# A graph network on Trainium2: gathered rows added by two engines, SiLU gives the slot back, and a new order of the stages

## The chip, the cores and the metric

The kernel runs on one core of a Trainium2 chip. The metric is the device time of one execution in microseconds (us). The engines are named as in the profile: PE (TensorE, matmuls; PEld are its weight loads), DVE (VectorE), ACT (ScalarE), POOL (GpSimd) and SP (SyncE, which starts DMAs).

## What is computed

Two layers of message passing on a graph of 6250 nodes with 128 features and 100000 edges, sorted by destination. Layer 1 is the part that matters here:

```python
src, dst = (edge_index[0], edge_index[1])
msg_input = jnp.concatenate([h[src], h[dst], edge_feat], axis=-1)
messages = jax.nn.silu(msg_input @ W1 + b1) @ W2 + b2
agg = jax.ops.segment_sum(messages, dst, num_segments=h.shape[0])
upd_in = jnp.concatenate([h, agg], axis=-1)
h_new = jax.nn.silu(upd_in @ W3 + b3) @ W4 + b4
return h_new + h
```

The result is added to x and normalised (a layer norm). Layer 2 sums x[src] over the edges of each node, sends the sum through a small network and normalises again. All of it is float32.

## The kernel before

**Tiling.** Nodes lie in 49 tiles of 128. Edges lie in 196 groups of 512, and two groups make a pair: 98 pairs. The product h @ W1 for the source part is computed once for all nodes and stored in memory as a table (src_term); a group's 512 rows of it are then gathered by four indirect DMAs of 128 rows (`gather_rows`, L866 to L871) into one of eight slots of `gath`. Slots 2m and 2m+1 hold the two groups of a pair, so gathers may run four pairs ahead.

**One pair.** SP loads the destinations and the edge features (`load_pair`, L699). POOL starts the eight gathers (`gather_sources`, L873); for each group it first waits until the slot is free, which is `pre_ps` of the group eight before. PE turns the edge features (`turn_ef`, L1187) and ACT copies them into `terms_l` and `terms_r` (`edge_features`, L1005 and L1006); ACT also copies the window of the destinations' features (`window_x`, L995), which the next `turn_ef` needs. DVE makes the 0/1 matrix of destinations (`windows`, L1885, also into `terms_l`). PE's `pre_sums` (L1197) then forms, for each of the two groups, the input of SiLU in its own PSUM bank (`bank[0]`, `bank[1]`): four matmuls (L1206) for the destination and edge parts, and one matmul with the identity (L1210, 128x512) that adds the gathered rows. A matmul is two instructions. ACT's `messages(0)` and `messages(1)` (L1009, L1014) apply SiLU to each bank and write `msg`. DVE makes `oh` (`one_hots`, L1618), PE sums the messages by destination (`message_sums`, L1220 and L1222), and DVE adds those sums into S and T (`add_sums`, L1896 to L1900).

**One unit.** Every second step one tile of nodes goes through the update: PE `hidden0` (L1230 to L1232), ACT `hidden0` (SiLU, L1023), PE `out0` (L1242), DVE `rows0` (L2014 to L1987), ACT `std0` (a square root, L1027), DVE `norm0` (L1992, L1998), ACT `store0` (L1048), PE `turn_x1` (L1255), ACT `start_T` (L1053). SiLU and the square root need different function tables, so ACT loads a table where they alternate (the ACT_TABLE_LOAD rows of L1023 and L1027).

**Order.** Each engine runs its own program. `steps` (L473) writes it: in step s a stage with lag n works on pair s - n (`of_pair(n, ...)`), on a unit every second step (`of_unit(n, ...)`), or on an early group (`of_early`), and within a step the stages stand in the order in which they are given to `steps`. Four steps make one loop body. While DVE sorts the edges for layer 2 (`sort_edges`, L1802, in steps 1 to 44), with PE turning keys in twelve of those steps, the steps are written out one by one. After that the early stages prepare layer 2 beside the pairs (`early_rows` L1353, `early_sums` L1366 on PE, `keep_early` L1060 on ACT, `early_hots` and `add_early` on DVE). The orders are in the calls of `steps` on SP (L822), ACT (L1114), PE (L1484) and DVE (L2130), and POOL's in `skewed` (L948). Engines meet through counting semaphores: `done(n)` is the count after item n.

Layer 2 starts when the last normalised tile of layer 1 is stored. Its gathers share the line L869.

Of the kernel before, what the change touches and what calls it, by code (L numbers as in the profile page):

```python
# [14 lines left out]
D = 128  # L15
# [41 lines left out]
def build(nc, x, src, dst, ef, W1, b1, W2, b2, W3, b3, W4, b4, eps, V1, c1, V2, c2, gamma, beta, out):  # L57
# [36 lines left out]
    with ExitStack() as ctx:  # L94
# [232 lines left out]
        pre_ps = counter("pre_ps", "pe")  # L327
        msg_made = counter("msg_made", "act")
# [296 lines left out]
        def in_banks(lag, body):  # L625

            return [of_unit_in(0, FIRST_BEFORE, lag, lambda j: body(j, bank[6])),
                    of_unit_in(FIRST_BEFORE, UNITS - 1, lag, lambda j: body(j, bank[2])),
                    of_unit_in(UNITS - 1, UNITS, lag, lambda j: body(j, bank[0]))]
# [9 lines left out]
        FIRST_BEFORE = (FIRST_EARLY + 3 - 8) // 2  # L639
# [27 lines left out]
        def _(sp):  # L667
# [155 lines left out]
            steps(sp, NPAIR - 2, (1, SORTED, SORTED + 1, SORTED + 2), of_unit(9, load_unit0), of_pair(0, load_pair),  # L823
# [5 lines left out]
        def _(pool):  # L829
# [43 lines left out]
            def gather_sources(k, u, t):  # L873
# [3 lines left out]
                for g in (2 * k, 2 * k + 1):  # L877
                    if g >= RING:
                        pool.wait_ge(pre_ps, done(g - RING))
                    gather_rows(A_d, N, g % RING, src_col[:, g * CH:(g + 1) * CH], gathered[g % RING])  # L880

            def gather_bridge(k):
# [4 lines left out]
                for h in range(2):  # L887
                    g = 2 * k + h
                    pool.wait_ge(pre_ps, done(g - RING))
# [60 lines left out]
            skewed(NPAIR + BRIDGED, [(0, gather_sources), (9, rsqrt0_of)])  # L950
# [3 lines left out]
        def _(act):  # L954
# [153 lines left out]
            def any_order():  # L1108
# [13 lines left out]
        def _(pe):  # L1122
# [39 lines left out]
            def sum_misfits():  # L1162
                pe.wait_ge(misfits_made, 6)
                pe.wait_ge(sums_added, done(SORTED - 4))
                mm(bank[2 + SORTED % 2][0:1, XW:XW + 6], ones[:, 0:1], misfits[:, :],
# [31 lines left out]
            def pre_sums(k, m, q):  # L1197
# [63 lines left out]
            def sort_bank(s):  # L1261

                pe.wait_ge(sums_added, done(s - 4))
                return bank[2 + s % 2]
# [74 lines left out]

            def hnew_read(j):  # L1340

                pe.wait_ge(v_made, done(j))
# [127 lines left out]
            def any_order():  # L1470
                for x in range(BRIDGED):
# [22 lines left out]
        def _(dve):  # L1494
# [236 lines left out]
            def take_columns(s, h, n):  # L1731
# [4 lines left out]
                                bank[2 + s % 2][:, XW:XW + 2 * ROWS].rearrange("p (c r) -> p c r", c=2)) \  # L1736
# [3 lines left out]
            def take_rows(s, h, n, b):  # L1740
# [3 lines left out]
                ve_.tensor_scalar(key_rows[:, h * XW:(h + 1) * XW], bank[2 + s % 2][0:ROWS, XW:2 * XW],  # L1744
# [22 lines left out]
            def take_chunks(s, h, n):  # L1767
# [3 lines left out]
                ve_.tensor_copy(src_chunks[:, h * XW:(h + 1) * XW], bank[2 + s % 2][:, XW:2 * XW]) \  # L1771
# [22 lines left out]
            def count_misfits():  # L1794

                dve.wait_ge(misfits_summed, 1)
                ve_.tensor_reduce(misfit_sum[:, :], bank[2 + SORTED % 2][0:1, XW:XW + 6], AX_X, ALU.add) \
# [361 lines left out]
```

## Time and profile before

| | us |
|---|---|
| three runs | 1912.32, 1918.95, 1919.72 |
| median | 1918.95 |
| profiled execution | 1915.15 |
| its span in the profile | 1913.0 |
| mean granted clock of PE | 0.874 |
| layer 1's steps, first stretch (sorting) | 141 to 631 |
| layer 1's steps, second stretch | 643 to 1256 |
| layer 2 starts | 1322 |

The profile lists, for each engine and line, how long instructions were busy, and behind a bar or in brackets how long the engine had stood idle just before, and what ended that: a named engine and line, "issue" (nothing that the profile shows), or "remote" (a semaphore whose sender isn't found). The ends of PE's records are modelled, not observed.

### The profile page before, as it was taken

The numbers are of one execution on the slowest core, as the hardware profiler recorded it, in microseconds if no ns is written. First come the engines' busy times: TensorE is split into PE (matmuls) and PEld (weight loads), VectorE is DVE, ScalarE is ACT, GpSimd is POOL, SyncE is SP. The second block draws the span as 40 slices with busy tenths as digits, with TensorE's granted clock in tenths as the row PEclk, the third lists the DMA queues.
The fourth block names the chain that finished last, engine by engine and source line by source line (L and its number), as shares of the span: only waits on it lengthen the run. The fifth ranks groups of instructions, "written<-read, shape, count | busy, mean of one in ns | idle before, by whom it ended". The sixth has DMA issues, their size and how long they took to land.

```text
span 1913.0 us, 31192 instructions
## 1 busy us (share of the span) xinstructions
PE 1449.5 (76%) x8093; PEld 1148.8 (60%) x8093; DVE 1016.9 (53%) x2306; ACT 631.5 (33%) x1257; POOL 1102.2 (58%) x1164
## 2 busy tenths in 40 slices
PE   5357777777777778777777777886488888888893
PEld 5245555555555556566565565664377777777773
DVE  5137775565654444445444454444245656766666
ACT  4223444444444444444444444342001111111110
POOL 2656666666666666565565555662366666666640
PEclk8677888888888899899899888888699999999996
DMA  5222232232335334343333333322466666656631
GB/s 187 73 53 73 77 79 76 78 81 74 80 83 96 93 97 106 100 101 99 100 98 101 98 97 102 100 71 77 138 190 184 177 181 184 186 176 190 186 104 30
DMA packets 189123, 214.13 MB, mean 112 GB/s; under 512 B 60426, under 2 KB 149517, under 8 KB 189011
## 3 DMA queue, kind: packets, MB, share of 16 engines
q1 hardware_dynamic: 138399, 131.62, 23.0%
q0 software_dynamic: 36352, 74.52, 16.3%
q10 hardware_dynamic: 14260, 6.68, 1.2%
q8 instruction: 48, 0.79, 0.2%
q14 instruction: 64, 0.52, 0.1%
HBM read 202.74 MB, written 9.85 MB: 111 GB/s over the span
## 4 chain that ended last, share of the span: by engine, by line
PE 31%; another core or an unknown queue 29%; issue 19%; ACT 10%; DVE 5%; ACTq 3%; DVEq 1%; SPq 1%; DMA 1%; POOLq 0%; POOL 0%
PE bank L1404 5%; PE bank L1206 5%; PE bank L1210 4%; PE bank L1380 4%; PE bank L1220 4%; ACT msg L1014 2%; PE bank L1353 2%; ACTq L994 2%; PE bank L1332 2%; ACT L1027 1%; PE bank L1366 1%; ACT terms_r L1006 1%; ACT terms_l L1005 1%; ACT S L1068 1%
## 5 line engine op out<-in xcount | busy, mean ns | idle before, releaser
L869 POOL DMA_INDIRECT gath<-src_term,src_col x784 | 752.1, 959 | 479.8 <-issue 211.0
L869 POOL DMA_INDIRECT gath<-layer_input,src_col x336 | 326.2, 971 | 210.8 <-PE bank L1332 105.0
L1206 PEld LDWEIGHTS bank<-terms_r,terms_l 128*128 128x128 f32 x1568 | 250.4, 228 | 193.5 <-issue 191.4
L1206 PE MATMUL bank<-terms_r,terms_l 128*128 128x128 f32 x1568 | 270.0, 316 | 119.6 <-issue 112.1
L1220 PE MATMUL bank<-oh,msg 128*128 128x128 f32 x1568 | 227.8, 293 | 100.8 <-issue 84.0
L1220 PEld LDWEIGHTS bank<-oh,msg 128*128 128x128 f32 x1568 | 212.6, 206 | 145.5 <-issue 118.7
L1210 PE MATMUL bank<-gath,ident 128*128 128x512 f32 x392 | 242.9, 701 | 19.6 <-issue 19.4
L1896 DVE TENSOR_TENSOR S<-S,bank 128x128 f32 x98 | 28.2, 288 | 416.6 <-remote 279.6
L1885 DVE TENSOR_SCALAR_CACHE_REDUCE terms_l<-dst_bc,node_col 64x512 f32<-64x512 int32 x196 | 222.0, 1133 | 41.4 <-issue 35.5
L1404 PE MATMUL bank<-S 128*128 128x288 f32 x672 | 193.9, 443 | 37.3 <-ACT S L1068 28.3
L1404 PEld LDWEIGHTS bank<-S 128*128 128x128 f32 x672 | 136.9, 209 | 86.7 <-issue 47.5
L1068 ACT COPY S<-bank 128x512 f32<-128x512 f32 x84 | 46.5, 588 | 382.8 <-remote 288.5
L1618 DVE TENSOR_TENSOR oh<-bank,dst_rel 128x1024 f32<-128x1024 f32 x140 | 170.0, 1214 | 0.0
L1005 ACT COPY terms_l<-bank 64x512 f32<-64x512 f32 x196 | 113.2, 578 | 158.6 <-remote 131.1
L1014 ACT ACTIVATE msg<-bank 128x512 f32<-128x512 f32 x196 | 112.4, 597 | 81.9 <-remote 55.3
L1955 DVE TENSOR_TENSOR S<-bank,dst_of 128x2304 f32<-128x2304 f32 x44 | 112.3, 2553 | 47.6 <-issue 27.3
L1332 PE MATMUL bank<-oh,gath 128*128 128x128 f32 x672 | 100.7, 287 | 45.1 <-issue 42.6
L1332 PEld LDWEIGHTS bank<-oh,gath 128*128 128x128 f32 x672 | 87.1, 198 | 50.3 <-issue 50.0
L1006 ACT COPY terms_r<-bank 64x512 f32<-64x512 f32 x196 | 113.7, 580 | 0.0
L1023 ACT ACT_TABLE_LOAD x47 | 60.3, 1283 | 132.2 <-remote 100.2
L1353 PEld LDWEIGHTS bank<-xs,xTs 128*128 128x128 f32 x384 | 52.9, 206 | 70.5 <-issue 70.3
L1210 PEld LDWEIGHTS bank<-gath,ident 128*128 128x128 f32 x392 | 72.9, 227 | 31.5 <-issue 31.5
(208 smaller groups left out, 1768.9 us busy)
## 6 DMA issues: line engine op xcount, KB each, us to landing
dst_bc<-in_dst SPq DMA_DIRECT2D x195, 128.0 KB
xT<-sorted_src SPq DMA_DIRECT2D x42, 512.0 KB
xs<-layer_input SPq DMA_DIRECT2D x136, 128.0 KB
gath<-src_term,src_col POOLq DMA_INDIRECT x784
terms_l<-layer_input SPq DMA_DIRECT2D x88, 128.0 KB
terms_r<-layer_input SPq DMA_DIRECT2D x88, 128.0 KB
msg<-layer_input SPq DMA_DIRECT2D x80, 128.0 KB
ef_s<-in_edge_attr SPq DMA_DIRECT2D x97, 64.0 KB
```

The source lines that it names most:

```text
L869: g.indirect_dma_start(out=gath[:, slot, j * D:(j + 1) * D], out_offset=None, in_=table[0:rows, :], in_offset=bass.IndirectOffsetOnAxis(ap ...
L1005: a.copy(terms_l[r, u, h, :, :], bank[4][r, 0:P].unsqueeze(1).to_broadcast([W, CH, P]))
L1006: last = a.copy(terms_r[r, u, 1 - h, :, :], bank[4][r, P:2 * P].unsqueeze(1).to_broadcast([W, CH, P]))
L1014: a.activation(msg[:, 2 * (m % 2) + h, :], bank[h][:, :], ACT.Silu).then_inc(msg_made, 1)
L1206: mm(bank[h][:, j * D:(j + 1) * D], terms_l[:, u, h, j, :], terms_r[:, u, h, j, :], start=j == 0, stop=False)
L1210: mm(bank[h][:, :], ident[:, :], gath[:, slot, :], start=False, stop=True).then_inc(pre_ps, 1)
L1220: mm(bank[2 + u][:, 0:PW], msg[:, 2 * u + c // CH, c % CH * D:(c % CH + 1) * D], oh[:, u, c, :], start=c == 0, stop=c == 2 * CH - 1)
L1332: last = mm(bank[2 + u][:, 0:PW], gath[:, s, c % CH * D:(c % CH + 1) * D], oh[:, u, c, :], start=c == 0, stop=c == 2 * CH - 1)
L1404: last = mm(bank[4][:, 0:DW], rows_kept[:, c // CH, c % CH * D:(c % CH + 1) * D], dst_hot[:, u, c, :], start=o % LATE == 0 and c == 0, sto ...
L1618: ve_.tensor_tensor(oh[:, u, :, :], iota_ps.unsqueeze(1).to_broadcast(shape), dst_rel[:, ds((k + first) * (2 * CH), 2 * CH)].unsqueeze(2). ...
L1885: ve_.tensor_scalar(terms_l[r, u, h, :, :], dst_bc[r, u, :].rearrange("n (p j) -> n j p", j=CH), node_col[r, ds(k, 1)], None, ALU.is_equal ...
L1955: ve_.tensor_tensor(hot, iota1_ps.unsqueeze(1).to_broadcast(shape), dst_of[:, ds(first, count)].unsqueeze(2).to_broadcast(shape), ALU.is_e ...
```

## The change

- For the second group of a pair PE no longer multiplies the gathered rows by the identity. A new DVE stage `add_gathered` adds `bank[1]` to the rows in the slot, and SiLU of the second group reads the slot. The first group stays as it was. `pre_ps` still counts both groups; for the second it now stands behind the four matmuls.
- POOL waits for `msg_made` (SiLU done) where it waited for `pre_ps`, for both slots.
- The unit stages run two steps later on every engine. ACT's `std0` moves from the end of the step to a place ahead of `messages(0)`. DVE's `add_sums` runs one step later and stands ahead of `windows`. PE's `early_sums` stands ahead of `early_rows`; `hnew_read` is gone, because `out0` writes to half of `bank[3]` instead of `bank[2]`. Sorting uses the other bank of the two.

```diff
             for g in (2 * k, 2 * k + 1):
                 if g >= RING:
-                    pool.wait_ge(pre_ps, done(g - RING))
+                    pool.wait_ge(msg_made, done(g - RING))
...
                 g = 2 * k + h
-                act.wait_ge(pre_ps, done(g))
+                if h == 0:
+                    act.wait_ge(pre_ps, done(g))
+                else:
+                    act.wait_ge(pre_made, done(k))
                 act.wait_ge(sums_ps, done(k - 2))
-                a.activation(msg[:, 2 * (m % 2) + h, :], bank[h][:, :],
+                a.activation(msg[:, 2 * (m % 2) + h, :], bank[0][:, :] if h == 0 else gath[:, 2 * m + 1, :],
                              ACT.Silu).then_inc(msg_made, 1)
...
-              of_unit(8, hidden0), of_unit(10, store0), of_unit(11, start_T),
-              of_pair(1, edge_features), of_pair(0, window_x), of_pair(2, messages(0)),
-              of_early(2, keep_early), of_pair(2, messages(1)),
-              of_unit(9, lambda j: None if rsqrt_on_pool(j) else std0(j)))
+              of_unit(10, hidden0), of_unit(12, store0), of_unit(13, start_T),
+              of_pair(1, edge_features), of_pair(0, window_x),
+              of_unit(11, lambda j: None if rsqrt_on_pool(j) else std0(j)),
+              of_pair(2, messages(0)), of_early(2, keep_early), of_pair(2, messages(1)))
...
-                pe.wait_ge(msg_made, done(g - 2))
+                if h == 0:
+                    pe.wait_ge(msg_made, done(g - 2))
+                else:
+                    pe.wait_ge(pre_made, done(k - 1))
                 for j in range(CH):
-                    mm(bank[h][:, j * D:(j + 1) * D], terms_l[:, u, h, j, :], terms_r[:, u, h, j, :],
-                       start=j == 0, stop=False)
-                slot = 2 * m + h
-                pe.wait_ge(gathered[slot], 16 * CH * (q + 1))
-                mm(bank[h][:, :], ident[:, :], gath[:, slot, :], start=False, stop=True).then_inc(pre_ps, 1)
+                    last = mm(bank[h][:, j * D:(j + 1) * D], terms_l[:, u, h, j, :], terms_r[:, u, h, j, :],
+                              start=j == 0 or h == 1, stop=h == 1)
+                if h == 0:
+                    pe.wait_ge(gathered[2 * m], 16 * CH * (q + 1))
+                    last = mm(bank[0][:, :], ident[:, :], gath[:, 2 * m, :], start=False, stop=True)
+                last.then_inc(pre_ps, 1)
...
-              of_early(3, early_kept), of_pair(1, turn_ef), of_pair(2, pre_sums), of_early(2, early_rows),
-              of_early(3, early_sums), (0, NPAIR, keys_taken),
-              of_unit_in(FIRST_BEFORE, UNITS - 1, 9, hnew_read), of_pair(3, message_sums),
+              of_early(3, early_kept), of_pair(1, turn_ef), of_pair(2, pre_sums), of_early(3, early_sums),
+              of_early(2, early_rows), (0, NPAIR, keys_taken), of_pair(3, message_sums),
               at_steps({4: weight_products}),
-              of_unit(10, ordered_turn_x1), *in_banks(8, ordered_out0), of_unit(7, ordered_hidden0),
+              of_unit(12, ordered_turn_x1), *in_banks(10, ordered_out0), of_unit(9, ordered_hidden0),
...
+        def add_gathered(k, m, q):
+
+            slot = 2 * m + 1
+            dve.wait_ge(gathered[slot], 16 * CH * (q + 1))
+            dve.wait_ge(pre_ps, done(2 * k + 1))
+            ve_.tensor_tensor(gath[:, slot, :], bank[1][:, :], gath[:, slot, :], ALU.add).then_inc(pre_made, 1)
...
-        steps(dve, NPAIR - 2, range(1, SORTED + 2), at_steps({5: weight_products}), *in_banks(9, rows0),
-              of_early(4, add_early), of_pair(1, windows), of_pair(2, one_hots(0, sums_ps, oh_made)),
-              of_unit(9, ordered_norm0), of_pair(3, add_sums), (0, NPAIR, sort_edges),
-              of_early(1, early_hots))
+        steps(dve, NPAIR - 2, range(1, SORTED + 2), at_steps({5: weight_products}), *in_banks(11, rows0),
+              of_early(4, add_early), of_pair(4, add_sums), of_pair(1, windows),
+              of_pair(2, one_hots(0, sums_ps, oh_made)),
+              of_pair(2, add_gathered), of_unit(11, ordered_norm0), (0, NPAIR, sort_edges), of_early(1, early_hots))
```

## Rows read from the trace of the kernel before

**Rows 1.** The page, busy us of each engine, share of the span, instructions.
```profile
PE 1449.5 (76%) x8093; PEld 1148.8 (60%) x8093; DVE 1016.9 (53%) x2306; ACT 631.5 (33%) x1257; POOL 1102.2 (58%) x1164
```

**Rows 2.** The page, the chain of work that ended last, by engine.
```profile
PE 31%; another core or an unknown queue 29%; issue 19%; ACT 10%; DVE 5%; ACTq 3%; DVEq 1%; SPq 1%; DMA 1%; POOLq 0%; POOL 0%
```

**Rows 3.** Stretches: window and length, busy us (instructions) of each engine, PE clock, DMA.
```profile
141.00:631.00 490.00, 374.31 (x1876) 279.81 (x1877) 296.08 (x744) 216.03 (x425) 315.11 (x329) 0.84 0.32 80
643.00:1256.00 613.00, 481.52 (x2688) 368.10 (x2689) 286.38 (x658) 267.10 (x540) 360.17 (x376) 0.91 0.38 100
1322.00:1363.00 41.00, 14.27 (x64) 11.35 (x64) 14.70 (x11) 0.00 (x0) 30.96 (x32) 0.67 0.47 139
```

**Rows 4.** Gathers (L869), 141 to 631: durations, starts; then idle us before, times.
```profile
L869 POOL DMA_INDIRECT gath<-src_term,src_col x329: 952/958/1293, 141.6 to 630.9; - x165
...
  remote: 86.5, 41
```

**Rows 5.** The same view of the stretch 643 to 1256.
```profile
L869 POOL DMA_INDIRECT gath<-src_term,src_col x376: 952/958/1085, 642.8 to 1254.1; - x188
...
  PE bank L1210: 128.6, 36
```

**Rows 6.** Timeline, 319 to 345: start, us, engine, line, operation [idle before <-releaser].
```profile
319.54 0.58 ACT L1005 COPY terms_l<-bank 64x512 f32<-64x512 f32 x1 [6.52 <-remote]
319.86 0.96 POOL L869 DMA_INDIRECT gath<-src_term,src_col  x1 [2.11 <-remote]
...
322.12 1.09 ACT L1014 ACTIVATE msg<-bank 128x512 f32<-128x512 f32 x2
...
324.52 0.29 ACT L1027 ACTIVATE std<-mv,eps_col 128x1 f32<-128x1 f32 x1
...
324.83 1.28 ACT L1023 ACT_TABLE_LOAD   x1
...
328.00 1.02 PE L1210 MATMUL bank<-gath,ident 128*128 128x512 f32 x2
328.69 0.96 POOL L869 DMA_INDIRECT gath<-src_term,src_col  x1 [0.30 <-issue]
...
331.36 0.55 DVE L1735 COPY dst_rows_f<-bank 128x224 f32<-128x224 f32 x1 [3.34 <-remote]
331.42 0.58 ACT L1005 COPY terms_l<-bank 64x512 f32<-64x512 f32 x1 [1.91 <-remote]
331.69 0.96 POOL L869 DMA_INDIRECT gath<-src_term,src_col  x1 [2.04 <-remote]
```

**Rows 7.** The same view of the stretch 1153 to 1180.
```profile
1162.73 0.96 POOL L869 DMA_INDIRECT gath<-src_term,src_col  x1 [0.30 <-issue]
...
1165.67 0.29 DVE L1896 TENSOR_TENSOR S<-S,bank 128x128 f32 x1 [4.21 <-remote]
1165.70 1.28 ACT L1023 ACT_TABLE_LOAD   x1 [5.06 <-remote]
...
1168.48 0.96 POOL L869 DMA_INDIRECT gath<-src_term,src_col  x1 [4.79 <-PE bank L1210]
```

**Rows 8.** The same view, around 1362, the end of layer 2's first gathers.
```profile
1361.61 0.94 POOL L869 DMA_INDIRECT gath<-layer_input,src_col  x1 [0.30 <-issue]
1367.27 1.07 ACT L1068 COPY S<-bank 128x512 f32<-128x512 f32 x2 [46.75 <-remote]
1367.42 1.42 DVE L1949 TENSOR_SCALAR xT<-xT,even_odd 128x1024 f32<-128x1024 f32 x2 [20.03 <-remote]
```

**Rows 9.** Groups, whole span: busy us, mean ns | idle us before, releasers.
```profile
L1210 PE MATMUL bank<-gath,ident 128*128 128x512 f32 x392 | 242.9, 701 | 19.6 <-issue 19.4
L1014 ACT ACTIVATE msg<-bank 128x512 f32<-128x512 f32 x196 | 112.4, 597 | 81.9 <-remote 55.3 <-issue 14.5 <-PE bank L1210 10.0
L1023 ACT ACT_TABLE_LOAD x47 | 60.3, 1283 | 132.2 <-remote 100.2 <-issue 31.7
L1515 DVE TENSOR_TENSOR T<-bank,b_bc 128x512 f32<-128x512 f32 x12 | 8.1, 685 | 5.1 <-PE bank L1152 5.1
```

**Rows 10.** Timeline, 1299 to 1325: the last two units' update on PE.
```profile
1303.05 0.49 PE L1230 MATMUL bank<-xT,w 128*128 128x128 f32 x2
...
1310.04 0.70 PE L1230 MATMUL bank<-xT,w 128*128 128x256 f32 x2 [2.67 <-DVE v L2018]
```

More of the change, by code:

```diff
@@ L327, in build @@
         pre_ps = counter("pre_ps", "pe")
+        pre_made = counter("pre_made", "dve")
         msg_made = counter("msg_made", "act")
@@ L627, in in_banks @@
             return [of_unit_in(0, FIRST_BEFORE, lag, lambda j: body(j, bank[6])),
-                    of_unit_in(FIRST_BEFORE, UNITS - 1, lag, lambda j: body(j, bank[2])),
+                    of_unit_in(FIRST_BEFORE, UNITS - 1, lag, lambda j: body(j, bank[3][:, XW:2 * XW])),
                     of_unit_in(UNITS - 1, UNITS, lag, lambda j: body(j, bank[0]))]
@@ L638, in build @@
         FIRST_EARLY = SORTED + 2
-        FIRST_BEFORE = (FIRST_EARLY + 3 - 8) // 2
+        FIRST_BEFORE = (FIRST_EARLY + 3 - 10) // 2
         TURNS = (21, 22, 24, 25, 28, 29, 31, 32, 35, 36, 40, 41)
@@ L822, in _ @@
             sp.wait_ge(consts, 1)
-            steps(sp, NPAIR - 2, (1, SORTED, SORTED + 1, SORTED + 2), of_unit(9, load_unit0), of_pair(0, load_pair),
+            steps(sp, NPAIR - 2, (1, SORTED, SORTED + 1, SORTED + 2), of_unit(11, load_unit0), of_pair(0, load_pair),
                   at_steps({1: load_weights, SORTED: store_chunks, SORTED + 1: load_bases,
@@ L888, in gather_bridge @@
                     g = 2 * k + h
-                    pool.wait_ge(pre_ps, done(g - RING))
+                    pool.wait_ge(msg_made, done(g - RING))
                     gather_rows(x1_d, EARLY_TILES * P, g % RING, bridge_rows[:, k - NPAIR, h * CH:(h + 1) * CH],
@@ L949, in _ @@
             pool.wait_ge(src_ready, 1)
-            skewed(NPAIR + BRIDGED, [(0, gather_sources), (9, rsqrt0_of)])
+            skewed(NPAIR + BRIDGED, [(0, gather_sources), (11, rsqrt0_of)])
             either_order(pool, ordered1, any_order)
@@ L1163, in sum_misfits @@
                 pe.wait_ge(misfits_made, 6)
-                pe.wait_ge(sums_added, done(SORTED - 4))
-                mm(bank[2 + SORTED % 2][0:1, XW:XW + 6], ones[:, 0:1], misfits[:, :],
+                pe.wait_ge(sums_added, done(SORTED - 5))
+                mm(bank[3 - SORTED % 2][0:1, XW:XW + 6], ones[:, 0:1], misfits[:, :],
                    start=True, stop=True).then_inc(misfits_summed, 1)
@@ L1261, in sort_bank @@
             def sort_bank(s):
-                pe.wait_ge(sums_added, done(s - 4))
-                return bank[2 + s % 2]
+                pe.wait_ge(sums_added, done(s - 5))
+                return bank[3 - s % 2]
             def keys_to_columns(s, h, run):
@@ L1338, in early_kept @@
                 pe.wait_ge(rows_kept_made, done(e))
-            def hnew_read(j):
-                pe.wait_ge(v_made, done(j))
             def early_rows(e, m, q):
@@ L1735, in take_columns @@
                 ve_.tensor_copy(key_cols.rearrange("p (r c) -> p c r", c=CH)[:, 2 * h:2 * h + 2, :],
-                                bank[2 + s % 2][:, XW:XW + 2 * ROWS].rearrange("p (c r) -> p c r", c=2)) \
+                                bank[3 - s % 2][:, XW:XW + 2 * ROWS].rearrange("p (c r) -> p c r", c=2)) \
                     .then_inc(keys_read, 1)
@@ L1743, in take_rows @@
                 dve.wait_ge(keys_turned, n)
-                ve_.tensor_scalar(key_rows[:, h * XW:(h + 1) * XW], bank[2 + s % 2][0:ROWS, XW:2 * XW],
+                ve_.tensor_scalar(key_rows[:, h * XW:(h + 1) * XW], bank[3 - s % 2][0:ROWS, XW:2 * XW],
                                   sign[:, b:b + 1], None, ALU.mult).then_inc(keys_read, 1)
@@ L1770, in take_chunks @@
                 dve.wait_ge(keys_turned, n)
-                ve_.tensor_copy(src_chunks[:, h * XW:(h + 1) * XW], bank[2 + s % 2][:, XW:2 * XW]) \
+                ve_.tensor_copy(src_chunks[:, h * XW:(h + 1) * XW], bank[3 - s % 2][:, XW:2 * XW]) \
                     .then_inc(keys_read, 1)
@@ L1796, in count_misfits @@
                 dve.wait_ge(misfits_summed, 1)
-                ve_.tensor_reduce(misfit_sum[:, :], bank[2 + SORTED % 2][0:1, XW:XW + 6], AX_X, ALU.add) \
+                ve_.tensor_reduce(misfit_sum[:, :], bank[3 - SORTED % 2][0:1, XW:XW + 6], AX_X, ALU.add) \
                     .then_inc(misfits_added, 1)
@@ L1871, in sort_edges @@
                 elif s == SORTED + 1:
+                    dve.wait_ge(oh_made, done(SORTED - 1))
                     ve_.tensor_copy(iota1_ps, iota_w[:, :]).then_inc(iota1_kept, 1)
```

## The prediction

> **What bounds the kernel now.** I read the busy shares and the chain first [rows 1, 2]. No engine is full: TensorE 76%, GpSimd 58%, VectorE 53%, ScalarE 33%; the chain is spread over TensorE lines, with 29% on a queue the profile can't name. Such a chain says that the work goes round a loop of engines, so I read the first layer's steps as a loop. Two stretches make up most of that layer: A, 141 to 631 us, where VectorE also sorts, and B, 643 to 1256 us, where ScalarE and TensorE also prepare layer 2 [rows 3].
>
> The gathers give the clock. In A GpSimd makes 329 gathers from 141.6 to 630.9, that is 41 bursts of 8 and one more: (630.9 - 141.6) / 41 = 11.93 us a pair. In 41 of them it waited 86.5 us, 2.11 us each [rows 4]. In B the last of 376 starts at 1254.1, the first of its burst 7 x 1.26 earlier, so (1245.3 - 642.8) / 46 = 13.1 us a pair, with waits for the fused group of L1210 of 128.6 us in 36 bursts, 3.6 us each [rows 5]. A burst itself is 8 x (0.96 + 0.30) - 0.30 = 9.8 us.
>
> What ends the wait? In A the burst from 319.86 ends its last issue at 328.69 + 0.96 = 329.65. At 331.36 VectorE, at 331.42 ScalarE and at 331.69 GpSimd all wake within 0.33 us of each other, after waits of 3.34, 1.91 and 2.04 us, though TensorE's records of both fused groups had ended at 329.02 [rows 6]. B shows the same at 1165.67 and 1165.70, 1.98 us after the last issue ended at 1163.69 [rows 7]. So TensorE's results are made known about 1.7 to 2.0 us after the last gather of a burst is issued, about 11.5 us after the burst began, whatever their records say. I call this moment F. At the start of layer 2, 32 gathers without a pause [rows 3] keep ScalarE waiting 46.75 us and VectorE 20.03 us until 1367.27, 4.7 us after the last one ended at 1362.55 [rows 8]: the same at four times the size. The records carry no cause for it.
>
> The Trainium skill (Perfetto Trace Analysis, Tensor Engine Instruction) says that the end of a TensorE instruction in the profile is computed and that its semaphore comes only when PSUM has acknowledged. That fits the order of events above, but gives no length of time. These rows leave open whether TensorE works late or reports late.
>
> So a pair in A is 9.8 of gathers, 1.7 to F, 0.3 to 0.4 for GpSimd to start: 11.9. In B it is the same 11.9 and 1.2 more, where TensorE's fused group comes after F: at 1168.48 GpSimd had waited 4.79 us, 2.8 beyond F [rows 7].
>
> **Part 1, the slot is given back by SiLU.** Today the next burst starts when TensorE's first fused group of the pair is known. After the change both slots wait for ScalarE's SiLU. This puts ScalarE between F and the burst. The SiLU takes 0.60 us [rows 9]. Every second step, std0 now stands right ahead of the SiLU, so a table load of 1.28 us for SiLU [rows 9] comes too. Does the load hide in the wait? The load of L1023 at 1165.70 came after its wait of 5.06 us [rows 7]; the one at 324.83 ran early, and its ACTIVATE waited [rows 6]. I take the load as exposed: (0.60 + 0.60 + 1.28) / 2 = 1.24 us a pair; hidden it is 0.60.
>
> Today four edge copies and two window copies stand between F and the SiLU: from 319.54 to 322.12, 2.58 us, plus 0.60 for the SiLU [rows 6]. Left there, the burst would start 3.2 us after F instead of 0.3. I don't expect it to stay so: if the burst is late by 3.2, TensorE has 3.2 us in which it is not held, and the turning of the next edge features (which needs only the window copies) is known early. From then on the copies of the next pair are done before F and only the SiLU is left behind F. TensorE has the slack: 374.31 us in 41 pairs of A is 9.1 us a pair, against a loop of 11.9 [rows 3]. The condition is that TensorE has reached that turning; this is the weakest step of the forecast, and a rival below prices its failure.
>
> The Trainium skill (ScalarE: Activation LUTs, What ACT_TABLE_LOAD costs) gives about 2.66 us for a switch, with a drain of 1.38 behind the 1.28 load. The trace disagrees on what follows the load: at 324.52 the ACTIVATE starts 0.02 us after the load ended. By the page the mean of part 1 would be (0.60 + 0.60 + 2.66) / 2 = 1.93 us, 0.69 more in each of 88 pairs, and the sum +119 instead of +58 us; the trace's row is used.
>
> **Part 2, the fused add of the second group.** Removed: 196 matmul instructions (two per add) of 0.70 us busy by the group's mean [rows 9]; back to back a pair of them is 1.02 us [rows 6], so 1.0 us of TensorE a pair. Added: one VectorE add of 128x512 from PSUM, 98 in all; the nearest row is L1515 with the same shape, 0.685 us [rows 9]; between 0.29 (L1896, a quarter the size, [rows 7]) and 1.2 it would change nothing in the sum, since SiLU of the first group (0.60) runs beside it and only the burst start counts. VectorE has 296.08 of 490.00 us busy in A [rows 3]. Queued behind the add's wait are norm0, the sort step and early_hots; the sort step of A then begins after F, with some 11 us until the next one for 7.2 us of work a pair in all (296.08 / 41).
>
> In A TensorE is not late, so 1.0 us saved there is covered. In B TensorE is the later one by 1.2 us a pair. The 1.0 us saved, and the windows and one_hots which no longer stand behind add_sums' wait (4.21 us at 1165.67 [rows 7]), take this away, and SiLU puts 1.24 in its place: 13.1 - 1.2 + 1.24 = 13.1. Its bounds: 0.60 and no residual, -0.6 a pair; residual kept, +1.2.
>
> **Part 3, order and lags.** The extra lag of add_sums, the new banks and the removed wait of hnew_read take no instruction away and add none; they lie beside the gathers. The unit stages run two steps later, so one more unit is left when the pairs are done. In the tail the last two units' L1230 start at 1303.05 and 1310.04 [rows 10]: 7.0 us a unit. Bounds 0 (the stages overlap better) and 14 (both ends of the chain). Layer 2 (1322 on) is not touched.
>
> **Sum**, against the profiled execution of 1915.15 us (span 1913.0; 3.8 below the median of the three runs, 1918.95): A 41 x 1.24 = +51; B 47 x 0 = 0; tail +7: +58, that is 1973 us.
>
> **Rivals.**
> *Copies stay between F and the SiLU (slower still).* For: [rows 6] show exactly this order today, and in B the turning comes late in TensorE's step. Against: the slack above. Price: start at F + 3.2 in steps without std0, F + 6.0 in the others (sqrt load 1.28, std 0.29, SiLU load 1.28), mean 4.6, against 0.3: +4.3 a pair. In a third of the 88 pairs: about +90 more, 2060; in all, past 2200. It decides when TensorE's turning of the next pair isn't known before the burst starts.
>
> *TensorE really is slowed by its load, and less load ends it (faster).* If the results are late because TensorE works off a backlog, then 1.0 us fewer and earlier windows make the group known within the burst, ScalarE does its SiLU beside the gathers, and GpSimd doesn't pause for it. B then falls by the saved 1.0 us a pair, 47 us, A by nothing to its wait of 2.11 - 0.30 = 1.8 us for some pairs: say -5 (a tenth of A's pairs); tail +7: 1870. With all pauses gone (10.1 us a pair) it would be below 1750; against that stands that 41 of 41 bursts of A end in the same wait, light steps and full ones. For: B's waits on L1210.
> The Trainium skill (SBUF — State Buffer, Who interferes with whom) states that DMA doesn't contend with compute engines and TensorE never waits on another. By that rule gathers can't hold TensorE, and this rival, 1870, would be the likely one. The common waking at 331.4 and 1165.7 speaks against it here.
>
> *A and B cancel (same).* B gains 1.2 a pair since the residual goes and the table load hides (0.60 only): 47 x -0.6 = -28; A 41 x 0.60 = +25; tail +7: 1919. For: the load at 324.83.
>
> *The change doesn't do what it says* can't well be: the add and the waits are plain in the diff.
>
> **Numbers.** Forecast (slower by 1 to 5%) 0.42, time 1973; copies between 0.16; faster 0.28; cancelling 0.14. The likeliest case's own range is 1930 to 2010. The two slower cases sum to 0.58. For 8 in 10 I leave out times under 1870 (0.11) and over 2060 (0.09). A measurement of this kernel tells about 0.5% from no change, so faster 0.28, same 0.14, slower 0.58.
>
> **What would show it.** GpSimd's wait before each burst in A goes from 2.1 to 2.7 us in one step and 4.0 in the next, its releaser ScalarE's SiLU (L1014's successor); 4.6 or more a pair means the copies rival; a wait under 1.5 means that the group is known within the burst, and the forecast fails. In B L1210 no longer holds GpSimd. VectorE's wait at add_sums goes, and one at the new add comes. The new add has 98 records of about 0.69 us. The second layer starts about 58 us later than 1322. If VectorE's add starts over 2 us after ScalarE's first SiLU, VectorE is late, which I priced at nothing.

## The result

The changed kernel takes 2034.17 us (median of four runs, 2026.26 to 2043.88), the kernel before 1918.81 on the same chip: a ratio of 1.062, 95% interval 1.059 to 1.066. The forecast was 1973, slower, with a range to 2060: the direction and the place were right, the size was half. Forecast was +54 against the median, measured is +115.

The page of the changed kernel first: its span and busy shares, and the groups that answer to [rows 1] and [rows 9] (for L1018, from SBUF and then from PSUM).

```profile
span 2041.7 us, 30881 instructions
...
PE 1401.4 (69%) x7897; PEld 1148.3 (56%) x7897; DVE 1071.6 (52%) x2404; ACT 637.1 (31%) x1257; POOL 1100.6 (54%) x1164
...
L870 POOL DMA_INDIRECT gath<-src_term,src_col x784 | 750.2, 957 | 610.6 <-ACT msg L1018 380.7
...
L1018 ACT ACTIVATE msg<-gath 128x512 f32<-128x512 f32 x98 | 61.8, 631 | 268.9 <-DVE gath L1898 191.9
...
L1898 DVE TENSOR_TENSOR gath<-bank,gath 128x512 f32<-128x512 f32 x98 | 66.2, 675 | 84.1 <-remote 77.4
L1018 ACT ACTIVATE msg<-bank 128x512 f32<-128x512 f32 x98 | 58.6, 597 | 57.9 <-remote 36.7
```

No engine has more work that matters; every share of the span fell, because the span grew. GpSimd's idle time before gathers rose from 479.8 to 610.6 us, and 380.7 of it ends with the SiLU (L1018), for which it didn't wait before. The new add costs 0.675 us, as priced (0.685).

Next, the gathers of both stretches, in the view of [rows 4] and [rows 5].

```profile
L870 POOL DMA_INDIRECT gath<-src_term,src_col x329: 949/955/1246, 132.3 to 725.3; - x165
...
  ACT msg L1018: 185.4, 21
```

```profile
L870 POOL DMA_INDIRECT gath<-src_term,src_col x369: 949/955/1061, 748.4 to 1370.6; - x185
...
  ACT msg L1018: 167.3, 45
```

In the first stretch there are 21 waits of 8.8 us where there had been 41 of 2.1; that is 4.5 us a pair, at the edge of the 4.6 that the forecast named as the sign of its copies rival. There is a new rhythm: the bursts go two by two, 16 gathers without a pause and then a long gap. From pair 8 to pair 49 a pair takes 14.69 us (11.93 before), from pair 50 to 96 13.53 us (13.10 before). The difference of the two profiled executions, 2041.7 - 1913.0 = 128.7 us, is then 41 x 2.76 = +113 in the first stretch, 46 x 0.43 = +20 in the second, -8 ahead of them (pair 8 starts at 133.5 instead of 141.6), +5 between the stretches and in the tail, and -1 in layer 2 (590.9 and 590.1 us long).

One period of the rhythm, from the timeline (start, us, engine, line, operation, idle before):

```profile
440.77 0.95 POOL L870 DMA_INDIRECT gath<-src_term,src_col  x1 [9.47 <-ACT msg L1018]
441.12 0.67 DVE L1898 TENSOR_TENSOR gath<-bank,gath 128x512 f32<-128x512 f32 x1
...
441.61 1.02 PE L1217 MATMUL bank<-gath,ident 128*128 128x512 f32 x2
...
445.67 0.60 ACT L1018 ACTIVATE msg<-bank 128x512 f32<-128x512 f32 x1
...
447.48 0.38 PE L1199 MATMUL bank<-wab,xw 128*128 128x128 f32 x2
...
459.67 0.95 POOL L870 DMA_INDIRECT gath<-src_term,src_col  x1 [0.31 <-issue]
...
463.59 0.37 ACT L1057 ACTIVATE T<-bank,one_eps 128x128 f32 x1 [9.66 <-remote]
463.60 0.55 DVE L1738 COPY dst_rows_f<-bank 128x224 f32<-128x224 f32 x1 [10.34 <-remote]
463.85 0.57 ACT L1006 COPY terms_l<-bank 64x512 f32<-64x512 f32 x1
...
466.00 0.39 ACT L996 COPY xw<-xT 128x64 f32 x2
466.41 1.28 ACT L1031 ACT_TABLE_LOAD   x1
...
467.70 0.29 ACT L1031 ACTIVATE std<-mv,eps_col 128x1 f32<-128x1 f32 x1
...
468.02 1.28 ACT L1018 ACT_TABLE_LOAD   x1
...
469.31 0.60 ACT L1018 ACTIVATE msg<-bank 128x512 f32<-128x512 f32 x1
...
470.18 0.95 POOL L870 DMA_INDIRECT gath<-src_term,src_col  x1 [9.55 <-ACT msg L1018]
```

Read it from the bottom. GpSimd waited from 460.62 to 470.18. The first 2.97 us of that end at F (463.59), when ScalarE and VectorE wake together; TensorE's turning of the edge features had a record that ended at 447.86. Then ScalarE does everything that stands ahead of the SiLU: T 0.26, four copies and two window copies to 466.39, the load for the square root, std0, the load for SiLU, SiLU until 469.91: 6.3 us. GpSimd follows 0.27 later. The next pair's first SiLU runs at 445.67, five microseconds after the burst began and well before GpSimd asks for the slot at 450.85, so the second burst follows without a gap. What that SiLU reads, TensorE made at 441.61 (L1217), also after the burst had begun. So a result of TensorE does get through early in a burst. The trace's semaphore records, of which some are missing, say the same: from 440.77 TensorE's semaphores rise once more at 443.54 and then not until 463.39. Of the stretch's 20 double bursts 19 show none between 6 and 22.6 us after the first gather; the other shows one at 9.2. A period is 19.85 + 2.97 + 6.3 + 0.3 = 29.4 us for two pairs.

In the second stretch the bursts go two by two only in part, and many of the waits are at a place that the forecast didn't look at. Between pair 50 and pair 96, 24 waits for the SiLU stand before the first group's slot (73 us) and 22 before the second group's (97 us). In 14 of those 22 the second SiLU had itself just waited for VectorE's add. The longest kind looks like this:

```profile
1020.40 0.29 DVE L1907 TENSOR_TENSOR S<-S,bank 128x128 f32 x1 [8.86 <-issue]
...
1022.47 0.37 PE L1230 MATMUL bank<-ident,deg_col 128*1 128x128 f32 x1 [1.73 <-issue]
1022.50 0.21 DVE L1911 TENSOR_TENSOR T<-T,bank 1x64 f32 x1 [1.14 <-issue]
...
1026.30 0.68 DVE L1898 TENSOR_TENSOR gath<-bank,gath 128x512 f32<-128x512 f32 x1
...
1027.01 0.63 ACT L1018 ACTIVATE msg<-gath 128x512 f32<-128x512 f32 x1 [3.93 <-DVE gath L1898]
...
1027.91 0.95 POOL L870 DMA_INDIRECT gath<-src_term,src_col  x1 [7.55 <-ACT msg L1018]
```

VectorE stands in add_sums until TensorE's sums come (1022.50), then does windows and one_hots, and only then the add that gives the second slot back.

### The profile page after: what moved, and what is told of

It is laid out like the page before. It is cut to its first block, busy times and chain, and to the rows that moved or that the text cites. A ratio compares the mean times of both kernels' runs of the same rounds, so it can differ in the third digit from the quotient of the medians.

```text
span 2041.7 us, 30881 instructions
## 1 busy us (share of the span) xinstructions
PE 1401.4 (69%) x7897; PEld 1148.3 (56%) x7897; DVE 1071.6 (52%) x2404; ACT 637.1 (31%) x1257; POOL 1100.6 (54%) x1164
## 4 chain that ended last, share of the span: by engine, by line
another core or an unknown queue 28%; PE 21%; DVE 19%; issue 18%; DVEq 6%; SPq 4%; ACT 2%; DMA 1%; ACTq 1%; POOLq 0%; POOL 0%
DVEq L1902 5%; PE bank L1408 4%; DVE terms_l L1889 4%; PE bank L1213 3%; DVE oh L1621 3%; PE bank L1384 3%; PE bank L1228 2%; PE bank L1217 2%; DVE gath L1898 2%; DVE bank L1701 1%; DVE src_rows_f L1705 1%; PE bank L1340 1%; PE bank L1357 1%; DVE src_rows_f L1709 1%
## 5 line engine op out<-in xcount | busy, mean ns | idle before, releaser
L870 POOL DMA_INDIRECT gath<-src_term,src_col x784 | 750.2, 957 | 610.6 <-ACT msg L1018 380.7
L1213 PE MATMUL bank<-terms_r,terms_l 128*128 128x128 f32 x1568 | 286.6, 328 | 222.4 <-issue 192.1
L1213 PEld LDWEIGHTS bank<-terms_r,terms_l 128*128 128x128 f32 x1568 | 264.4, 240 | 303.6 <-issue 289.9
L1228 PE MATMUL bank<-oh,msg 128*128 128x128 f32 x1568 | 247.6, 314 | 116.0 <-issue 101.8
L1228 PEld LDWEIGHTS bank<-oh,msg 128*128 128x128 f32 x1568 | 229.4, 226 | 127.4 <-issue 107.0
L1907 DVE TENSOR_TENSOR S<-S,bank 128x128 f32 x98 | 28.3, 289 | 262.0 <-issue 227.1
L1018 ACT ACTIVATE msg<-gath 128x512 f32<-128x512 f32 x98 | 61.8, 631 | 268.9 <-DVE gath L1898 191.9
L1217 PE MATMUL bank<-gath,ident 128*128 128x512 f32 x196 | 136.9, 786 | 6.7 <-issue 6.5
L1898 DVE TENSOR_TENSOR gath<-bank,gath 128x512 f32<-128x512 f32 x98 | 66.2, 675 | 84.1 <-remote 77.4
L1057 ACT ACTIVATE T<-bank,one_eps 128x128 f32 (+2 forms) x48 | 17.4, 363 | 220.1 <-remote 210.4
L1018 ACT ACTIVATE msg<-bank 128x512 f32<-128x512 f32 x98 | 58.6, 597 | 57.9 <-remote 36.7
```

The costliest lines, as they stand in the source:

```text
L870: g.indirect_dma_start(out=gath[:, slot, j * D:(j + 1) * D], out_offset=None, in_=table[0:rows, :], in_offset=bass.IndirectOffsetOnAxis(ap ...
L1018: a.activation(msg[:, 2 * (m % 2) + h, :], bank[0][:, :] if h == 0 else gath[:, 2 * m + 1, :], ACT.Silu).then_inc(msg_made, 1)
L1213: last = mm(bank[h][:, j * D:(j + 1) * D], terms_l[:, u, h, j, :], terms_r[:, u, h, j, :], start=j == 0 or h == 1, stop=h == 1)
L1217: last = mm(bank[0][:, :], ident[:, :], gath[:, 2 * m, :], start=False, stop=True)
L1228: mm(bank[2 + u][:, 0:PW], msg[:, 2 * u + c // CH, c % CH * D:(c % CH + 1) * D], oh[:, u, c, :], start=c == 0, stop=c == 2 * CH - 1)
```

## The experiments

Two things were open: what in the change costs, and whether the held-back results are what makes it cost.

**The parts, each alone.** e1 changes GpSimd's waits alone, in this loop and in the same way in that of the early gathers:

```diff
-                        pool.wait_ge(pre_ps, done(g - RING))
+                        pool.wait_ge(msg_made, done(g - RING))
```

> The kernel before with one edit: GpSimd waits for msg_made (SiLU) instead of pre_ps, for both slots. TensorE still adds both groups, order and lags as before. Theory 1 (the slot given back by SiLU is what costs): ScalarE's four edge copies and two window copies (2.6 us) and the SiLU (0.6 us) stand between the moment F at which TensorE's results are known and the next burst. In the first stretch the bursts go two by two or start 3 us later; 13.0 to 15.0 us a pair instead of 11.9, and the whole kernel is 60 to 130 us slower than before. Theory 2 (the new order and the lags cost): within 20 us of before. Theory 3 (VectorE's add costs): within 20 us of before.

e2 is the changed kernel with TensorE adding both groups and GpSimd waiting for `pre_ps`.

> The changed kernel's order, lags and banks, but TensorE adds the gathered rows of both groups and GpSimd waits for pre_ps, as before. Theory 1: the first stretch stays at 11.9 us a pair (GpSimd does not wait for ScalarE), the second falls by up to the 1.2 us of TensorE's lateness; the whole is 0 to 50 us faster than before. Theory 2: at least 60 us slower than before. Theory 3: like theory 1.

e3 is the kernel before with VectorE's add in place of TensorE's for the second group, and this wait for the slots:

```diff
+                        pool.wait_ge(msg_made if h else pre_ps, done(g - RING))
```

> The kernel before, its order and lags, with VectorE's add for the second group alone. GpSimd waits for pre_ps for the first group's slot and for SiLU for the second group's (which SiLU reads). Theory 1: SiLU of the second group ends about 5 us after F, when the second half of a burst is due anyway (5.1 us after the first), so the first stretch stays near 12 us a pair and the whole is within 25 us of before. Theory 3 (the add on VectorE or ScalarE's wait for it costs): SiLU of the second group and with it TensorE's message sums come later, 30 us or more slower than before.

e4 is the changed kernel with that same wait.

> The changed kernel with one edit: for the first group's slot GpSimd waits for pre_ps again; the second group's slot still waits for SiLU. Theory 1: the burst starts 0.3 us after F, the rhythm of two bursts goes; the second half waits where std0 with its two table loads stands ahead (every second step, SiLU of the second group about 8 us after F, 2.8 us too late), so 12 to 13.5 us a pair in the first stretch, and the whole is 60 to 120 us faster than the changed kernel (2034), 1915 to 1975. Theory 2: within 30 us of the changed kernel.

Measured, on another chip: before 1516.85, e1 1517.78 (ratio 1.000, interval 0.999 to 1.001), e2 1521.84 (1.003, 1.002 to 1.004), e3 1517.53 (1.000, 0.999 to 1.001), e4 1519.91 (1.002, 1.001 to 1.003). The kernel before is 400 us faster here than at the prediction, with the same code, and no part costs 10 us. A pair takes 10.1 us in e1 and e2, where all the theories had started from 11.9, so the totals decide between none of them (e1 came out as theories 2 and 3 said and e3 as theory 1, but for want of the loop). So the next question was the chip, and the changed kernel itself went beside its parts.

> The changed kernel as it is, beside the kernel before on the chip of the experiments, where the kernel before took 1517 us and its gathers run without a pause. Theory 1 (what the change costs is SiLU between the moment at which held-back results of TensorE become known and the next burst): where nothing is held back, SiLU is long done when a slot is needed, so 10.1 us a pair in both kernels and within 10 us of before. Theory 4 (the change costs about 100 us wherever it runs): 1590 us or more.

Measured: 1518.84 against 1517.14, ratio 1.0016 (1.0006 to 1.0026). Its gathers from 141 to 1000 us, and a piece of its timeline from layer 2:

```profile
L870 POOL DMA_INDIRECT gath<-src_term,src_col x681: 951/955/1310, 141.2 to 999.8; - x171
...
  issue: 199.9, 656
  ACT msg L1018: 7.6, 25
```

```profile
1091.80 1.17 PE L1384 MATMUL bank<-xs,xT 128*128 128x128 f32 x9
...
1092.17 0.94 POOL L870 DMA_INDIRECT gath<-layer_input,src_col  x1 [0.30 <-issue]
...
1093.06 0.59 ACT L1072 COPY S<-bank 128x512 f32<-128x512 f32 x1 [6.92 <-PE bank L1384]
```

In layer 1 GpSimd never stops (0.30 between gathers), and a pair takes 10.10 us in e9 and in e1 alike. ScalarE, which had waited 6.92 us for TensorE, wakes at 1093.06, 0.09 us after TensorE's record ended and in the middle of the gathers. Nothing is seen to be held back here. The loop of the first traces isn't a property of the program alone. In five groups of runs the kernel before took 1516.85, 1517.14, 1517.32 and 1517.04 us on four occasions and 1946.2 us on one, with 1918.8 at the prediction. Why some runs hold and others don't isn't answered by any run here; each of these five groups had a chip of its own, so even that it goes with the chip is not shown.

**Holding by hand.** To test the loop on a chip that doesn't hold, ScalarE and VectorE were made to wait, at the head of each step, for the gathers in flight; where GpSimd waits for `pre_ps` it waits for them too:

```diff
+            def held(k, m, q):
+                for h in range(2):
+                    act.wait_ge(gathered[2 * ((m + 3) % STEPS) + h], 16 * CH * (q + (m + 3) // STEPS + 1))
...
-            steps(act, NPAIR - 2, range(STEPS), ...
+            steps(act, NPAIR - 2, range(STEPS), (2, NPAIR - 4, held), ...
```

> The kernel before, with the holding made by hand: ScalarE and VectorE wait at the head of step k + 2, and GpSimd ahead of each burst, until all gathers of pair k + 3 (the burst in flight) have landed. Theory 1: this rebuilds the loop of the first trace, about 11.8 us a pair, so layer 1 is some 160 us longer than on this chip without it: 1650 to 1720 us. If the loop is not what set the pace there, TensorE's work stays hidden and the pair takes another time.

> As h0_before_held, but GpSimd waits for SiLU (msg_made) for both slots, as in the change. Theory 1: edge copies, window copies and SiLU stand between the landing and the next burst: about 3 us a pair more than h0_before_held in most steps, 150 to 300 us longer than it. Theory 2 (order and lags cost): like h0_before_held.

> The changed kernel with the same holding by hand on ScalarE and VectorE (GpSimd waits for SiLU anyway). Theory 1: like h1_silu_held and 1.3 to 2.9 us more in every second step for std0 and its table loads; at least 150 us longer than h0_before_held. Theory 4 rival: the holding plays no part and the two differ as the unheld kernels do.

Measured: h0 1766.13, h1 2073.5, h2 2169.24 us, beside 1517.14. The pairs take 12.33 and 12.90 us in h0 (first and second stretch; 11.93 and 13.10 in the first trace), 15.82 and 15.90 in h1, 16.80 and 16.94 in h2. h0 missed its band (1650 to 1720 us, 11.8 us a pair); h1 lies 7 us outside its own (150 to 300 over h0). The pace of h0 is within 0.4 us of the first trace, but that is put in rather than found: a burst of 9.8 us whose landing all three engines must await sets it by itself. What these runs do test is the price of an edit where each burst waits for the landing: 307 us for the single edit of GpSimd's wait, 403 for the whole change. The holding by hand lets nothing pass during a burst, though, and the same change costs 115 us where the chip holds back by itself. One turn of h2, in a step with std0, ScalarE's and GpSimd's rows:

```profile
422.11 0.95 POOL L870 DMA_INDIRECT gath<-src_term,src_col  x1 [0.30 <-issue]
424.72 0.37 ACT L1062 ACTIVATE T<-bank,one_eps 128x128 f32 x1 [8.18 <-DMA gath<-src_term,src_col]
...
430.44 0.60 ACT L1023 ACTIVATE msg<-bank 128x512 f32<-128x512 f32 x1
431.31 0.95 POOL L870 DMA_INDIRECT gath<-src_term,src_col  x1 [8.25 <-ACT msg L1023]
```

From the landing at 424.72 to the end of SiLU are 6.3 us, the same as after 463.59 in the real one.

**The other parts under holding.** h3 is the order alone; h4 is h2 with std0 last in the step; h5 has both SiLUs ahead of the copies as well; h6 is h2 with `pre_ps` for the first slot, and GpSimd waits for the landing too, as in h0. Each of these took two executions.

> The changed kernel's order, lags and banks alone (TensorE adds both groups, GpSimd waits for pre_ps), with the holding by hand on ScalarE, VectorE and GpSimd as in h0_before_held (1766 us). Theory 1: GpSimd does not wait for ScalarE, so no more than 12.3 us a pair in both stretches and 1700 to 1770 us in all. Theory 2 (the order and the lags are what costs under holding): 1850 us or more.

> h2_after_held (2169 us) with one edit: std0 stands last in ScalarE's step again, as before the change. Theory 1: sqrt load 1.28, std 0.29 and SiLU load 1.28 leave the path in every second step, but hidden0 gets a table load of 1.28 back in the others: (1.57 + 1.28 - 1.28) / 2 = 0.8 us a pair, 70 us less than h2, about 2100; as h1_silu_held or up to 30 us above it.

> h2_after_held (2169 us) with one edit: ScalarE applies both SiLUs ahead of the edge and window copies, and std0 stands last. Theory 1: only hidden0 or start_T and the SiLU stand between the landing and the next burst; the 2.6 us of copies leave the path and the std0 loads too: 13.0 to 13.8 us a pair, 1820 to 1900 us in all. If ScalarE's place were not the cause (rival: TensorE or VectorE end the wait next), it stays above 2050.

> The changed kernel, GpSimd waiting for pre_ps for the first group's slot and for SiLU for the second's, with the holding by hand on all three engines. Theory 1: the first half of a burst starts 0.3 us after the landing; the second half, due 5.1 us later, waits for the second SiLU only in the steps with std0 (it ends some 7 us after the landing): 12.3 to 13.5 us a pair, 1750 to 1870 us, 300 us or more below h2_after_held. It measures what the wait for the first slot alone costs. Theory 3 (VectorE's add costs): 2000 us or more.

| | us | us a pair, first / second stretch |
|---|---|---|
| h0, before, held | 1766.13 | 12.33 / 12.90 |
| h3, order alone, held | 1785.57 | 12.40 / 13.05 |
| h6, changed, first slot early, held | 2016.83 | 14.86 / 15.60 |
| h4, changed, std0 last, held | 2117.55 | 15.93 / 16.36 |
| h5, changed, SiLU first, held | 2120.77 | 15.31 / 16.93 |
| h2, changed, held | 2169.24 | 16.80 / 16.94 |

The order is nearly free (h3 missed its band by 16 us and theory 2's by 64). Moving std0 back gives 52 us (70 expected). h6 gives 152, not 300, and h5 only 48, not 270: both came out as their rivals said, h6 above theory 3's 2000 us and h5 above 2050. Something else ends the wait there. The gathers of h6 in the first stretch show where, and its timeline what the SiLU waits for:

```profile
L870 POOL DMA_INDIRECT gath<-src_term,src_col x266: 949/955/964, 140.9 to 627.0; - x133
...
  ACT msg L1027: 92.6, 33
```

```profile
407.06 0.68 DVE L1907 TENSOR_TENSOR gath<-bank,gath 128x512 f32<-128x512 f32 x1
...
407.77 0.63 ACT L1027 ACTIVATE msg<-gath 128x512 f32<-128x512 f32 x1 [2.87 <-DVE gath L1907]
...
408.67 0.95 POOL L870 DMA_INDIRECT gath<-src_term,src_col  x1 [2.44 <-ACT msg L1027]
```

Each of 33 pairs waits 2.8 us for the second SiLU, and that SiLU waits for VectorE. VectorE's add is short, but it is queued behind add_sums, windows and one_hots. h9 moves it ahead of them:

```diff
...
-of_early(4, add_early), of_pair(4, add_sums), of_pair(1, windows),
-of_pair(2, one_hots(0, sums_ps, oh_made)), of_pair(2, add_gathered), ...
+of_early(4, add_early), of_pair(2, add_gathered), of_pair(4, add_sums), of_pair(1, windows),
+of_pair(2, one_hots(0, sums_ps, oh_made)), ...
```

> h6_first_slot_held (2017 us, 14.86 us a pair) with one edit: VectorE's add of the gathered rows stands ahead of add_sums, windows and one_hots. Theory 3b (in h6 the second slot comes back late because the add is queued behind about 4 us of other work on VectorE): the second SiLU ends 3 us earlier in the steps without std0 and the pair takes 12.8 to 13.8 us, 100 us or more less than h6. Theory 1 alone (ScalarE's copies and loads): within 30 us of h6.

Measured: 12.98 us a pair in the first stretch, 13.70 in the second, against 14.86 and 15.60 of h6. The waits for the second SiLU fall to 28.3 us in 16 pairs. This group ran where before takes 1946.2 us, so the totals (2005.41) can't be set beside h6's. The pace of the first layer can, with a caution: this chip may add holding of its own to that made by hand, which would hide a part of the gain and not make one.

**The rhythm of two.** h7 holds in every second step alone, h8 has std0 last besides.

> The changed kernel with the holding by hand in every second step alone (on ScalarE and VectorE, in the steps that have std0), so that bursts can go two by two as in the trace of the changed kernel. Theory 1 (bursts by two, then copies, std0 with its loads and SiLU after the landing): 16 gathers take 19.9 us, the landing 2 to 3, ScalarE 6.6: 14.2 to 14.9 us a pair, against 14.69 in that trace; 2.0 us a pair under h2_after_held, 1960 to 2030 us in all. If the rhythm of two isn't made by the long step, it stays near 16.8 us a pair.

> As h7_after_held_by_two, with std0 last in ScalarE's step. Theory 1: one step of two loses 2.85 us of std0 and its loads: 1.4 us a pair less than h7, about 13.0, 90 to 130 us less in all. If the loads are not what stands there, no difference.

Measured on that same chip: h7 14.82 us a pair in the first stretch (14.69 in the trace of the change), with gaps of mostly 9.8 to 10.1 us before every second burst; 2161.47 us in all. The total missed its band by 131 us; layer 2 takes 608 us of it, against 462 in h6. But h7 doesn't show that holding by hand makes the rhythm, because this chip holds back by itself: of 18 waits before `start_T` (L1062) 17 end with "remote", as all 18 do in the changed kernel, while in h2 all 15 end with the landing of the gathers. So h7 is nearer to the changed kernel seen once more on a second chip that holds back; the changed kernel itself wasn't run there. h8, against h7, then prices the place of std0 under the chip's own holding: 14.16 us a pair, 0.66 less where 1.4 was expected, and 2133.41 in all, 28 less where 90 to 130 were. In the second stretch the two are alike (15.34, 15.42).

**Less work for TensorE.** h10 is h0 without TensorE's add for the second group; the gathered rows of that group are left out of the computation. TensorE's wait for them now stands ahead of the group's four matmuls.

> h0_before_held (1766 us) without TensorE's add of the gathered rows of the second group; this part of the computation is left out. It measures what 1.0 us less of TensorE a pair is worth under holding, the gain that the prediction put into the second stretch. If that stretch is bounded by TensorE: 12.90 us a pair falls to 11.9 to 12.3 there, 30 to 50 us less in all. Rival: the pace is that of the landing and ScalarE, within 10 us of h0.

Measured: 1954.21 us, beside 1946.2 for before without holding by hand on the same chip (ratio 1.002, 0.997 to 1.006). Its pairs take 12.40 and 13.36 us; h0's took 12.33 and 12.90. GpSimd in the second stretch:

```profile
L869 POOL DMA_INDIRECT gath<-src_term,src_col x368: 950/956/1063, 643.8 to 1254.8; - x184
...
  PE bank L1220: 107.0, 28
```

It still waits 3.8 us for the group that TensorE adds (L1220), 28 times. No gain is seen, but h0 wasn't run on this chip, and where it ran TensorE was seldom the late one: there 12 waits of this stretch end with TensorE (41 us) and 35 with the landing (85 us), here 40 end with TensorE (141 us). So h10 can't tell what a microsecond less of TensorE is worth; it shows that on a chip that holds back TensorE's result is the later one even with less work.

**Once more alone.** Two kernels were run again on another chip.

> The same kernel as e1_wait_silu (the kernel before, GpSimd waiting for SiLU for both slots), once more, in case the chip is one that holds back (the kernel before near 1920 to 1950 us there). Theory 1: 13 to 15 us a pair in the first stretch, 60 to 130 us over before. Rival (only the whole change costs, through std0 and the add): within 25 us of before. On a chip that doesn't hold back (before near 1517): no difference.

> The same kernel as e4_first_slot_early (the changed kernel with pre_ps again for the first group's slot), once more, in case the chip holds back. Theory 1 with what h6 and h9 showed (the second slot comes back late behind VectorE's add): 12.3 to 14.0 us a pair in the first stretch, 20 to 80 us over before, against 100 to 120 for the whole change. Rival (the slot's release is not what costs): as the whole change, 100 us or more over before.

Before took 1517.04 there, s1 1516.93 (1.000, 0.999 to 1.001), s2 1519.35 (1.0015, 1.0006 to 1.0025). So the edit alone was never timed on a chip that holds by itself; its price under holding rests on h1, which is held by hand.

## Why the prediction was right or wrong

**Right: the loop, and where the change enters it.** GpSimd's wait moves to the SiLU, behind a moment F at which ScalarE and VectorE wake together; the price of the add and a layer 2 that stays as it was are in the trace. F itself is put too strictly. It describes most of the long waits, but in the kernel before results of TensorE also come in mid-burst: with gathers from 331.69 on, ScalarE wakes at 337.56 for a result of 336.19, and TensorE's semaphores rise between 3 and 9.8 us after the first gather in 39 of the 42 bursts of the first stretch.

```profile
336.19 0.47 PE L1255 MATMUL bank<-ident,ot 128*128 128x128 f32 x1
...
337.56 0.37 ACT L1053 ACTIVATE T<-bank,one_eps 128x128 f32 x1 [2.48 <-PE bank L1255]
```

**Wrong: "only the SiLU is left behind F".** This is the step that failed, the one called the weakest, and the term is the 1.24 us a pair of the first stretch: measured is 2.76, +113 us where +51 was forecast. The copies did stay ahead of the SiLU in the long step, and so did both table loads and std0, of which the term had one load. The prediction's rival priced this step as 6.0 us and the trace has 6.3. But the rival set 3.2 us for the other step, which would have given +4.3 a pair, and h2, 4.5 over h0, is that case. The real loop did a third thing: by the time GpSimd's wait of 9.5 us was over, TensorE had the next pair's inputs; its group got through in the first microseconds of the burst, ScalarE did its SiLU in mid-burst, and the next burst followed at once. So one step of two costs 6.3 and the other nothing, and the double burst holds longer (2.97 us after the last issue instead of 1.7). The prediction asked whether a longer pause lets TensorE tell the next result early, and answered it for the turning alone; it didn't follow what GpSimd then does with a slot that is free ahead of time. That 2034 lies inside the stated range is in part luck: the upper end was the price of the copies rival in a third of the pairs, which isn't what happened.

**Wrong: "the residual of the second stretch goes".** The 1.2 us a pair was put down to TensorE's load and to windows behind add_sums, and its end was to pay for the SiLU. It came out at +0.43 a pair, +20 us instead of 0. Two things are in it. The new order doesn't take the residual away: h3 keeps 13.05 (held by hand; h10, with 1.0 us less of TensorE, decides nothing, as said). And the prediction put "VectorE is late" at nothing, with the sign that its add would start over 2 us after the first SiLU; at 452.59 it starts 6.9 us after it. In the first stretch that costs nothing, since the slot isn't due until 455.89. In the second, 97 of the 171 us of waits for the SiLU are for the slot that the add gives back. h6 against h9 shows the same under holding by hand. How much of the +20 us is the add's place and how much the SiLU's was not isolated there.

**Mis-sized, small.** The tail was priced at +7; between the stretches and in the tail it is +5 together. The start of the first stretch gained 8, which no term had.

**The table load.** The Trainium skill (ScalarE: Activation LUTs, What ACT_TABLE_LOAD costs) would add a drain of 1.38 us. In the changed kernel the ACTIVATE starts at 469.31, 0.01 us after the load from 468.02 ended: no such drain. Where the loads stand does cost: h4 gives back 52 of h2's 403 us, and h8 0.66 us a pair against h7.

**The rival "TensorE is slowed by its load".** The change takes load from TensorE (1449.5 to 1401.4 us busy) and is slower, so the rival's time is refuted, and its mechanism stays open. The Trainium skill (SBUF — State Buffer, Who interferes with whom) says that a DMA never contends with a compute engine. The runs at 1517 us agree; those at 1919 and 1946 leave it open. There TensorE isn't only reported late: in the second stretch of the kernel before, neighbouring matmuls of L1206 start 1.0 to 2.6 us apart 74 times, in e1's trace once, and in the changed kernel's rows of the second stretch above, one of L1230 starts after 1.73 us in which the profile shows nothing to wait for. Whether that is contention, or something that keeps the instructions or their semaphores, no run here tells.

## What to carry to other kernels

Before giving a buffer back at a later point of the chain, list what the releasing engine does in program order ahead of that point, with its table loads, and check whether the ring has slack for it: here the same edit costs nothing where the ring runs ahead (e1) and 307 us where each burst is made to wait for the landing (h1 against h0). A short instruction moved to another engine costs its place in that engine's queue, not its duration (h6 against h9, and 1026.30 in the changed kernel). A loop that waits for something the profile can't name can be imitated by hand, with explicit waits, to rank the edits; the prices are those of the imitation (403 us against 115), and the run must stand on a chip that doesn't already hold back.

## What the runs showed of the hardware

The same program took 1517 us in four groups of runs and 1919 to 1946 us in two, each time steady within 0.6%. In the slower kind, results of TensorE are late while gathers are in flight, though not all of them: several engines wake together 1.7 us after the last issue of 8 gathers and 2.97 after 16, and TensorE's matmuls stand up to some 2 us apart; early in a burst, and in the kernel before in mid-burst too, some results get through. In the faster kind ScalarE wakes 0.09 us after TensorE's record, in mid-burst. Layer 2 differs too (591 and 608 us of span against some 460). A comparison holds for the kind of runs it was made on: the change is 6.2% slower on the one and 0.2% slower on the other.
